# The second inverse level of a gated delta-rule layer, spread over four array quarters and two PSUM banks

## The reference

```python
def step(carry, x):
    S_f, S_s = carry
    qt, kt, vt, bt, fdt, sdt, fgt, sgt = x
    S_f = fdt[..., None, None] * S_f
    S_s = sdt[..., None, None] * S_s
    err_f = vt - jnp.einsum('bhk,bhkv->bhv', kt, S_f)
    err_s = vt - jnp.einsum('bhk,bhkv->bhv', kt, S_s)
    bkt = bt[..., None, None] * kt[..., :, None]
    S_f = S_f + bkt * err_f[..., None, :]
    S_s = S_s + bkt * err_s[..., None, :]
    S_fc = _cap(S_f + rf * S_s)
    S_sc = _cap(S_s + rf * S_f)
    ot = fgt[..., None] * jnp.einsum('bhk,bhkv->bhv', qt, S_fc) + sgt[..., None] * jnp.einsum('bhk,bhkv->bhv', qt, S_sc)
    return ((S_fc, S_sc), ot)
```

## Time and profile before

| | us |
|---|---|
| median of 3 runs | 3071.02 (3070.17 to 3073.48) |
| the profiled execution, its time | 3071.01 |
| its span | 3069.2 |
| first L1382 to last L1382 (128 chunks) | 1435.4 |
| one chunk | 11.13 (11.39 every fourth) |

### The profile page before, as it was taken

The page is one execution under the profiler, slowest core; times in us unless marked ns, Lnnn a source line. Parts: engine busy times, 40 slices in busy tenths (PEclk is TensorE's granted clock), DMA queues, the critical chain, the costliest instruction groups (busy, mean ns, idle before and its releaser), DMA issues. The chain is left out here.

```text
span 3069.2 us, 68844 instructions
## 1 busy us (share of the span) xinstructions
PE 2648.2 (86%) x24613; PEld 1773.4 (58%) x24613; DVE 2313.0 (75%) x4183; ACT 1602.5 (52%) x4014; POOL 1367.1 (45%) x2167
## 2 busy tenths in 40 slices
PE   0889996749999999999999999999573988888888
PEld 0654443637777777777777777777472932222223
DVE  8868887956868688786878878765786477877775
ACT  0459996853434444444444444444582645555555
POOL 1113233115756667676666757666555024211111
PEclk9989997978999999999999999999797979999999
DMA  2016656862242333224233322321684212111110
GB/s 63 1 69 241 242 246 250 251 193 45 41 89 67 61 70 81 55 61 88 67 61 70 81 53 63 81 67 49 239 275 141 76 32 39 25 28 25 22 22 28
DMA packets 459979, 288.37 MB, mean 94 GB/s; under 512 B 375251, under 2 KB 419859, under 8 KB 450835
## 3 DMA queue, kind: packets, MB, share of 16 engines
q1 hardware_dynamic: 450422, 254.56, 30.4%
q10 hardware_dynamic: 4608, 16.78, 1.8%
q0 software_dynamic: 4608, 12.59, 1.2%
HBM read 153.83 MB, written 129.99 MB: 92 GB/s over the span
## 5 line engine op out<-in xcount | busy, mean ns | idle before, releaser
L2535 DVE TENSOR_REDUCE mx<-banks 128x2 f32<-128x1024 f32 (+3 forms) x384 | 358.2, 956 | 106.7 <-PE banks L1979 84.3
L2240 ACT ACTIVATE probs<-banks 128x1024 f32<-128x1024 f32 (+3 forms) x384 | 307.1, 811 | 245.9 <-PE banks L2001 238.9
L1765 POOL TENSOR_SCALAR_AFFINE_SELECT probs<-probs 128x256 f32<-128x256 f32 x256 | 103.7, 407 | 524.9 <-ACT probs L2240 524.7
L874 POOL TENSOR_SCALAR xc<-xc,halves 128x64 f32<-128x64 f32 (+1 forms) x256 | 150.6, 588 | 268.4 <-DVE xc L1379 255.5
L1858 PE MATMUL banks<-wproj,xnT 128*128 128x512 f32 x512 | 264.7, 599 | 0.6 <-DVEq L497 0.6
L1180 ACT COPY ssm<-banks 16x64 f32<-16x64 f32 (+2 forms) x896 | 216.7, 242 | 50.1 <-PE banks L977 37.9
L1227 ACT COPY ah<-banks 128x768 f32<-128x768 f32 x128 | 102.3, 799 | 254.5 <-PE banks L1050 254.5
L1050 PE MATMUL banks<-stk,tw 128*128 128x192 f32 x1024 | 204.7, 344 | 0.5 <-DVE tw L1385 0.5
L2001 PE MATMUL banks<-q_less,k_parts 64*128 64x512 bf16 (+3 forms) x768 | 133.6, 345 | 80.9 <-DVE mx L2535 59.9
L2018 PE MATMUL banks<-probs,vaug 128*9 128x256 f32 (+3 forms) x1920 | 196.1, 450 | 0.0
L1218 ACT ACTIVATE nycv<-banks 128x512 f32<-128x512 f32 x128 | 76.5, 598 | 207.4 <-PE banks L1040 207.4
(11 more groups left out here) (368 smaller groups left out, 6762.2 us busy)
## 6 DMA issues: line engine op xcount, KB each, us to landing
proj_s<-prj SPq DMA_DIRECT2D x32, 2048.0 KB, 6.8
qkv_t<-proj_s SPq DMA_DIRECT2D x32, 1536.0 KB
ka<-proj_s ACTq DMA_DIRECT2D x32, 512.0 KB, 4.9
mem_s<-o_sb SPq DMA_DIRECT2D x32, 512.0 KB, 2.7
om<-mem_s SPq DMA_DIRECT2D x32, 512.0 KB, 4.0
om<-proj_s SPq DMA_DIRECT2D x32, 512.0 KB, 4.9
nblk_s<-ssa POOLq DMA_DIRECT2D x32, 256.0 KB, 4.4
blk_s<-res SPq DMA_DIRECT2D x16, 512.0 KB, 4.2
```

What stands on the lines that cost most here:

```text
L874: pool.tensor_scalar(inverse_of(k, lv + 1)[:, :, w:2 * w], inverse_of(k, lv), halves[:, lv, 1:2], None, ALU.mult).then_inc(half_set, 1)
L2240: act.activation(probs[:, s % 2, :, at:at + w], slot_of((kind, s, k))[:, :, 0:w], ACT.Exp, scale=D1 ** -0.5).then_inc(b_read, 1)
L2535: dve.tensor_reduce(mx[:, s % 2, c, :, t:t + 1].rearrange("p e a -> p (e a)"), slot_of((kind, s, k))[:, :, 0:w], AX, ALU.max).then_inc(a_r ...
```

## The change

At level 1 heads 2 and 3 stay on the diagonal of the array, and their products go to bank 1; heads 0 and 1 are put across it (rows 0 to 63 write partitions 64 to 127 and the other way round), into bank 0. A stage still has eight matmuls of the same size, ordered so that four in a row lie in four different quarters. The turned inverses of heads 0 and 1 are needed on the other partitions, so `turn_inverse` writes them straight into `ttu`, and issues four transposes of half the width at each level in place of two; `copy_turned` is gone. The copies of level 1 read two banks. The negated joining block is made by ScalarE (`keep_joined`, behind `keep_turned(k+1)`) and no more by VectorE. `ttu` is cleared once, and TensorE waits for that. At level 2 the heads are paired otherwise, with as many matmuls in the same quarters.

```diff
-        def products(k, lv, b):
-            at = (0, 256)[lv - 1]
-            return slot4(k)[0][:, at:at + 4 * (SUB << lv)]
+        def products1(k, e):
+            return slot4(k)[e][:, 0:64]
+        def updates1(k, e):
+            return slot4(k)[e][:, 64:128]
+        def across(k):
+            return [(m, m // 2, m % 2) for m in (0, 2, 1, 3)]
...
+            pool.memset(ttu[:, :, :, :], 0.0).then_inc(zero_set, 1)
...
-            pe.wait_ge(zero_set, 5)
+            pe.wait_ge(zero_set, 6)
...
-                for m, h, r, p in heads(k) if lv == 1 else ():
-                    for out_, rows, right in quarters(lv):
-                        last = pe.matmul(products(k, lv, out_)[right, w * m:w * m + w], ssm[rows, lv, m, right], inverse_of(k, lv)[rows, m, :], start=True, stop=True)
+                for m, e, p in across(k) if lv == 1 else ():
+                    for b, rows in enumerate(HALVES):
+                        put = rows if e else HALVES[1 - b]
+                        last = pe.matmul(products1(k, e)[put, w * p:w * p + w], ssm[rows, lv, m, rows], inverse_of(k, lv)[rows, m, :], start=True, stop=True)
...
-                if lv == 2:
-                    pe.wait_ge(ttu_set, k + 1)
...
+                for m, e, p in across(k) if lv == 1 else ():
+                    for b, rows in enumerate(HALVES):
+                        src, turned = (rows, ttw[rows, k % 2, m, rows]) if e else (HALVES[1 - b], ttu[HALVES[1 - b], k % 2, p, :])
+                        last = pe.matmul(updates1(k, e)[rows, w * p:w * p + w], turned, xs[src, k % 2, w * m:w * m + w], start=True, stop=True)
...
-            def copy_turned(k):
-                act.wait_ge(ttw_set[1], k + 1)
+            def keep_joined(k):
+                act.wait_ge(u_mm[LEVELS - 1], k + 1)
+                act.wait_ge(half_set, 3 * k + LEVELS - 1)
                 if k >= 2:
-                    act.wait_ge(u_mm[LEVELS - 1], k - 1)
-                act.copy(ttu[HALVES[0], k % 2, :, :], ttw[HALVES[1], k % 2, 0:4:2, HALVES[1]]).then_inc(ttu_set, 1)
+                    act.wait_ge(am_mm, k - 1)
+                act.mul(tw[HALVES[1], k % 2, :, 0:64].rearrange("p (e q) t -> p e q t", e=2),
+                        span4(k, 0, 2)[HALVES[1], :].rearrange("p (e c) -> p e c", e=2)[:, :, 0:128].rearrange("p e (q t) -> p e q t", t=64), -1.0).then_inc(tw_set[LEVELS - 1], 1)
...
-                    copy_turned(k)
                     keep_lower(k, 2)
                 if more:
                     keep_turned(k + 1)
+                if new:
+                    keep_joined(k)
+                if more:
                     keep_factors(k + 1)
...
                 if lv == 0:
-                    dve.transpose(ttw[at[1], y, :, at[1]], xc1[at[1], y, :, :])
-                    dve.transpose(ttw[at[3], y, :, at[3]], xc1[at[3], y, :, :]).then_inc(ttw_set[0], 1)
+                    dve.transpose(ttw[at[1], y, 2:4, at[1]], xc1[at[1], y, 2:4, :])
+                    dve.transpose(ttu[at[3], y, :, own[1]], xc1[at[1], y, 0:2, :])
+                    dve.transpose(ttw[at[3], y, 2:4, at[3]], xc1[at[3], y, 2:4, :])
+                    dve.transpose(ttu[at[1], y, :, own[1]], xc1[at[3], y, 0:2, :]).then_inc(ttw_set[0], 1)
...
-                if new:
-                    keep_update(k, 2)
```

More of the change, by code:

```diff
@@ L663, in closed, with pairs1 @@
             return slot4(k)[e][HALVES[1], 0:128]
-        def quarters(lv):
-            return [(0, HALVES[0], HALVES[1])] if lv == LEVELS - 1 else [(b, HALVES[b], HALVES[b]) for b in range(2)]
-        def products(k, lv, b):
-            at = (0, 256)[lv - 1]
-            return slot4(k)[0][:, at:at + 4 * (SUB << lv)]
-        def updates(k, lv, b):
-            at = (128, 0)[lv - 1]
-            return slot4(k)[0][:, at:at + 4 * (SUB << lv)]
+        def products1(k, e):
+            return slot4(k)[e][:, 0:64]
+        def updates1(k, e):
+            return slot4(k)[e][:, 64:128]
+        def pairs1(k, at):
+            return span4(k, 0, 2).rearrange("p (e c) -> p e c", e=2)[:, :, at:at + 64]
+        def across(k):
+            return [(m, m // 2, m % 2) for m in (0, 2, 1, 3)]
         def span4(k, first_bank, banks_):
@@ L1020, in update @@
                         last = pe.matmul(updates0(k)[rows, :], xt0[:, k // 4 % 2, k % 4, half_, :], xs0[:, k % 2, 1 - half_, :], start=True, stop=True)
-                if lv == 2:
-                    pe.wait_ge(ttu_set, k + 1)
[L1023 to L1027, removed]
-                    for out_, rows, right in quarters(lv):
-                        last = pe.matmul(updates(k, lv, out_)[right, w * m:w * m + w], turned[right, right], xs[right, k % 2, w * m:w * m + w], start=True, stop=True)
+                for m, e, p in across(k) if lv == 2 else ():
+                    turned = ttw[HALVES[1], k % 2, m, HALVES[1]] if e else ttu[HALVES[0], k % 2, p, :]
+                    last = pe.matmul(closed(k, e)[:, w * p:w * p + w], turned, xs[HALVES[e], k % 2, w * p:w * p + w], start=True, stop=True)
+                for m, e, p in across(k) if lv == 1 else ():
+                    for b, rows in enumerate(HALVES):
+                        src, turned = (rows, ttw[rows, k % 2, m, rows]) if e else (HALVES[1 - b], ttu[HALVES[1 - b], k % 2, p, :])
+                        last = pe.matmul(updates1(k, e)[rows, w * p:w * p + w], turned, xs[src, k % 2, w * m:w * m + w], start=True, stop=True)
                 last.then_inc(u_mm[lv], 1)
@@ L1193, in keep_lower @@
                 if lv == 1:
-                    last = act.copy(xs[:, k % 2, 0:4 * (SUB << lv)], products(k, lv, 0))
+                    last = act.copy(xs[:, k % 2, 0:4 * (SUB << lv)].rearrange("p (e c) -> p e c", e=2), pairs1(k, 0))
                 if lv == 2:
@@ L1395, in turn_inverse @@
                 at = [slice(2 * SUB * b, 2 * SUB * b + 2 * SUB) for b in range(4)]
+                own = at[0:2]
                 if lv == 0:
[L1397 to L1401 removed]
+                    dve.transpose(ttw[at[1], y, 2:4, at[1]], xc1[at[1], y, 2:4, :])
+                    dve.transpose(ttu[at[3], y, :, own[1]], xc1[at[1], y, 0:2, :])
+                    dve.transpose(ttw[at[3], y, 2:4, at[3]], xc1[at[3], y, 2:4, :])
+                    dve.transpose(ttu[at[1], y, :, own[1]], xc1[at[3], y, 0:2, :]).then_inc(ttw_set[0], 1)
+                else:
+                    dve.transpose(ttw[at[2], y, 2:4, at[2]], xc1[at[2], y, 2:4, :])
+                    dve.transpose(ttu[at[0], y, :, own[0]], xc1[at[2], y, 0:2, :])
+                    dve.transpose(ttw[at[2], y, 2:4, at[3]], xc2[at[3], y, 2:4, 0:2 * SUB])
+                    dve.transpose(ttu[at[0], y, :, own[1]], xc2[at[3], y, 0:2, 0:2 * SUB]).then_inc(ttw_set[1], 1)
             def sum_squares(k):
```

20 lines of the change are left out of this document (5 added, 15 removed).

## The result

The changed kernel takes 3155.11 us (median of 4 runs, 3150.68 to 3164.40); the kernel before took 3070.60 us in the same comparison (4 runs). The ratio is 1.0278, 95% interval 1.0260 to 1.0295: slower. The prediction said slower, and with 3087 us it missed the size by 68 us; 3155 lies outside its range of 3074 to 3119. The profiled execution of after is one of 3153.52 us (span 3151.8 us) against 3071.01 us before, so the profiles show a difference of 82.5 us.

A forecast was written before the change was run, and what follows sets the result against it. A ring through TensorE, ScalarE and VectorE to `factors` bounds the loop, with VectorE becoming its own bound. 112 x 0.16 = +17.9, 15 x -0.10 = -1.5, +0.2 and -0.5 give 3071.0 + 16.1 = 3087 us; range 3074 to 3119.

The forecast's parts named there:

- The ring and the slack of 0.54 us: Chunk loop: a TensorE, ScalarE and VectorE cycle sets the 11.13 us period; VectorE idles 0.54 us before L1382.
- Level one in four quarters, 0.23 us less for each stage: TensorE's `lower(k,1)` and `update(k,1)`: eight load steps become four, saving 0.23 us each, 0.47 us a chunk.
- Rival 2: TensorE level 1: four quarters don't run at once; `factors` comes 0.36 us later, time 3117 us; chance 0.12.
- What was said of the Trainium skill there: TensorE level 1: by its PSUM bank and weight-load rules, the changed stages would keep their eight steps.
- A transpose of 32x64 takes 233 ns, 0.25 us apart: VectorE's `turn_inverse`: four transposes take 0.98 us where two take 0.63, +0.36 us twice a chunk.
- Rival 1: VectorE's small transposes are cheap, under 213 ns: about 3058 us at 200 ns, 3016 at 151 ns; chance 0.13.
- Move to ScalarE, nothing: Joining update leaves VectorE for ScalarE: a copy of about 0.37 us, 0.45 us to spare before `solve`, costing nothing.
- L1382's start to L1455's end is 1.99 us now and 2.35 after.: VectorE's chain ahead of `factors`: the small transposes lengthen this stretch, putting `factors` at 2018.73 against 2018.58.
- The term of 0.16 us a chunk: Later `factors` from VectorE's longer chain, +0.15 to +0.18 us; over 112 chunks +17.9 us.
- The 0.47 us of TensorE lies before this wait and turns into idle time in front of L989.: TensorE's level 1 saving, 0.47 us a chunk, becomes waiting before `factors` and shortens nothing.
- check (d): Profile sign: TensorE's idle time before `factors` rises from 0.15 to about 0.5 us or more, released by `o_sb`.
- a fall of the clock: TensorE's clock falling in the loop would make the prediction wrong altogether; no size or chance was given.

## Why the prediction was wrong

Step by step, as it was put.

- *The ring and the slack of 0.54 us.* Right. The wait of L1382 for L1029 has nearly gone (5.5 us in 16 chunks), and the wait before `factors` carries the loss.
- *Level one in four quarters, 0.23 us less for each stage.* Right: 0.32 us against 0.54. The run with two wide transposes shows 52 us for it, with `copy_turned` gone, where VectorE doesn't take it back. Rival 2 (the quarters don't run at once) falls. What was said of the Trainium skill there (TensorEngine Tiling (Array Packing), section Restrictions and Gotchas) is settled by the same row: at level 1 the two row halves of a head write the two partition halves of one bank, and the first row of L1031 holds both of its loads within 0.14 us, the next row, for the other bank, 0.01 us later.
- *A transpose of 32x64 takes 233 ns, 0.25 us apart.* Right for this kernel: 232 to 241 ns. Rival 1 (under 213 ns) falls. The run with the transposes alone shows that they start only 0.17 us apart where the partitions stay the same. The prediction named such an overlap only as something that would make it wrong, and didn't ask when it occurs. Its price was right because this kernel changes the partitions each time; that part was luck.
- *Move to ScalarE, nothing.* Right: 0.38 us, 0.68 us ahead of `solve`, and 0.9997 when done alone.
- *"L1382's start to L1455's end is 1.99 us now and 2.35 after."* **The first step that failed.** It is 2.49 (2112.51 to 2115.00). The sum lengthened the chain by the transposes and took the duration of L1454 along unchanged, 0.50 us. That duration belongs to where the operation stood: just before GpSimd's copy. 0.36 us later it stands on the copy, and takes 0.635. The term of 0.16 us a chunk is in truth 11.44 - 11.13 = 0.31. Over 127 chunks the missing 0.135 us are 17 us. Where the state is cleared, I had 0.10 us less; the trace with extra matmuls has 11.20 us, 0.07 more.
- *"The 0.47 us of TensorE lies before this wait and turns into idle time in front of L989."* **The second step that failed, and the larger one.** The mechanism was right, and check (d) even asked for 0.5 us or more of idle time (it is 0.72). But the sum gave that idle time no price and kept TensorE at the upper clock level. The prediction named a fall of the clock only as what would make it wrong altogether, without a chance or a price. It cost 43.6 us.

The account: 16 us as forecast, 17 for the longer L1458, 44 for the clock are 77 of the 84.5 us. The remaining 7 us are spread. In the run with extra matmuls, laid chunk by chunk beside the kernel before, 26 chunks lose more than the 0.31 us of the others, 5 us more together; in 23 of them VectorE also builds inverse rows (where it starts a new inverse, 12.30 us instead of 11.46). The prediction had taken all chunks as alike. The chunks that clear the state lose 1 us together where it had a gain of 1.5. Why the chunks with inverse rows cost more wasn't tested. The three terms are also not independent: with the copy held back the clock fell less, so the 17 us of L1458 brought part of the 44 with them.

With both terms taken out by experiment the kernel stands at 3101 us, inside the range of the prediction, 14 us above its figure; in that run the later GpSimd work costs some 12 us that no kernel of the prediction had.

## What to carry to other kernels

When a change shifts an operation in time, look up what the partner engine runs beside it before and after, and read its duration as that of the pair. When a change turns work of a nearly full TensorE into idle time, that time isn't free: price the clock from the rows, and look first for a place where the work can stay spread out, or the wait be shortened. Whether the time is lost there can be tried with a harmless repetition of matmuls in the gap: here more work made the kernel 44 us faster.

## What the runs showed of the hardware

**The clock and short waits.** The mean wait of TensorE before `factors` (where the table of waits gives it), and the falls of the clock in the loop, over the runs:

| kernel | wait before `factors`, us | falls | low, us |
|---|---|---|---|
| before | 0.15 | 1 | 10.2 |
| changed, two wide transposes | 0.32 | 1 | 6.8 |
| changed, extra matmuls | 0.25 | 1 | 10.2 |
| changed, copy held back | 0.51 | 10 | 44.4 |
| changed | 0.72 | 31 | 122.9 |
| changed, order of the heads | 0.72 | 22 | 81.9 |
| changed, copy of keys ahead | 1.18 | 105 | 382 |
| before, late `o_sb` | 1.45 | 125 | 525.6 |

I had not expected that waits well under one microsecond, in a loop in which TensorE is busy over 90% of the time (1417.97 of 1524.12 us), bring it to the lower level in a quarter of the chunks. The wait doesn't settle the number by itself: 0.72 us goes with 31 falls in one profile and with 22 in another. Why one chunk falls and its like does not, these runs don't show.

**VectorE and GpSimd.** An addition of VectorE whose two inputs both lie in SBUF (L1458, 128x256) has many lengths: 0.42 or 0.50 us beside nothing but the scaling (L877, before L874), 0.64 with a copy starting in it, 1.17 with the squares of the state, 1.34 with copy and squares. Beside the scaling alone it goes by the distance from that operation's start: 0.50 us in the 126 chunks of before in which it starts 0.25 us after it, 0.42 us where it starts 0.37 us after it (the transposes alone) or 0.61 us (the copy held back). L1459, the same size with one input in PSUM, takes 0.42 us in all of these kernels. The Trainium skill, SBUF — State Buffer, section "SBUF: two separate sides", says that a VectorE operation with two SBUF inputs and a GpSimd operation that reads SBUF share one pair of ports, which whoever starts first holds to its end while the other blocks. The rows agree on who collides: L1458 but not L1459. They don't agree on who waits: L904 starts 0.28 us after L1458 (2206.70 and 2206.42), keeps its 0.61 us, and it is L1458, the first, that becomes 0.75 us longer. With the copy both become longer in the changed kernel (0.64 and 0.63 us), where it starts 0.26 us into L1458; in the kernel with the late `o_sb`, where it starts 0.09 us into the second addition, the copy keeps its 0.39 us. Why a distance makes that difference stays open.

**Transposes on VectorE.** Two of 32x64 with the same partitions in and out start 0.17 us apart and overlap. Where the second reads or writes other partitions, it starts 0.01 to 0.02 us after the first has ended: 0.25 us apart in the changed kernel, 0.21 where the first itself overlapped (L1403 and L1404 of the transposes alone, 0.19 us and then 2015.34).
